# A selective-scan kernel: 64-step blocks for the drive, high channels first, softplus steps spread, delta spread by six reads

## The chip, the cores and the metric

The kernel runs on one core of one Trainium2 chip. The time is device microseconds of one execution. Lower is better.

## The reference

The model has two layers over 8 images of 64 x 64 x 96. The first is a group norm, an input projection to 192 channels and a gate, a 3 x 3 depthwise convolution with SiLU, and a selective scan in four directions (k): along two diagonal orders of the pixels and their reverses. The second is linear attention and a feed-forward layer in quantized arithmetic. The change touches the scan alone:

```python
delta = softplus(dts + dt_projs_bias)            # per k: 192 channels, 4096 steps
def step(hst, inp):                              # hst: 4 x 192 channels x 16 states
    u_t, d_t, B_t, C_t = inp
    hst = hst * exp(d_t[..., None] * A) + (d_t * u_t)[..., None] * B_t[:, :, None, :]
    return (hst, einsum('bkdn,bkn->bkd', hst, C_t))
```

## The kernel before

Each image goes through stages; a barrier of all engines (`rendezvous`) stands between them. The scan stage has four passes, one for each direction, of 8 chunks of T = 512 steps: 256 chunks in all. In a chunk the 192 x 16 states are 3072 rows of 512, cut into 12 *steps* s of 2 x 128 rows. A step takes one group of CW = 32 channels (GROUPS[s], six groups) and half of the 16 states (pr = s // 6; NJ = 4 quadrants of 32 partitions with 2 states, index a, each).

A step s consists of
- `decays` (ScalarE, L650): two exponentials of `delta_rep[:, g, :]`, where delta of the group's 32 channels stands four times, once in each quadrant. It is issued two steps ahead;
- `fill` (TensorE, L856): the drive delta x u x B of the step, by matmuls into two of four PSUM banks. The stationary operand is `du_t` (delta x u, turned so that time lies on partitions), the moving one `b_diag`, in which B stands on a diagonal. It is 32 matmuls, 64 instructions, in tiles of 64 rows by 32 columns. It is issued two steps ahead and waits for the scan of step s - 2, whose banks it writes;
- four `tensor_tensor_scan` (VectorE, L1144), halves of 256 steps for a = 0, 1;
- `save_state` (ScalarE, L632), then the product with C (GpSimdE, L487), which waits for that copy;
- `sum_states` (TensorE, L886), in batches of four steps, into the Y banks 4 and 5. Its place in TensorE's order is SUM_SLOTS.

While chunk ch runs, the next one, nx, is prepared, by calls written by hand into each engine's loop over s: `project` (TensorE, L819, L820: delta before softplus, and B and C), `copy_bc`, `clamp_exp`, `square_log` (ScalarE), `softplus_part` and `times_u` (GpSimdE, L463, L471), `at_least_log` and `make_delta` (VectorE, L1109, L1115), `turn_b`, `turn_du` (TensorE, L829, L838), `save_bt`, `save_du` (ScalarE, L606, L614). Each exists twice, v = 0 for the 64 high channels (DLO:DI) with B and C, v = 1 for the 128 low ones. Each engine works in order, so a call that waits holds up all behind it.

`prepare` is SyncE's list of DMAs for nx, also in order: C to DRAM, B to DRAM by four stores (L368), delta's high rows (L375), the reads of B's first half (L384), C's first half (L391), delta's low rows (L406), then 12 reads of delta (L401, 32 partitions each), B's and C's second halves. In `b_runs` each step's 8 values are 32 bytes of a row of 512 elements, and a shifted window over the rows gives the diagonal. Time is interleaved: block k of a half holds the steps t with t mod 4 = k (`every`).

## Time and profile before

| | us |
|---|---|
| median of 3 runs | 16174.73 (16163.91 to 16176.15) |
| the profiled execution | 16179.37 |
| its span | 16176.9 |

| engine | busy us | share of the span |
|---|---|---|
| TensorE, matmuls | 12939.1 | 80% |
| VectorE | 9552.7 | 59% |
| GpSimdE | 8899.6 | 55% |
| ScalarE | 7503.2 | 46% |

The shares are means over all stages. The scan stage shows in the page's slices as three to four of every five slices, with TensorE at 8, VectorE and GpSimdE at 6 tenths. In the rows below PE is TensorE, PEld its weight loads, DVE VectorE, ACT ScalarE, POOL GpSimdE, SPq the DMA queue of SyncE. L487 is line 487 of the kernel. All on-chip working buffers of the scan are parts of one tensor, `arena`, so rows are told apart by their lines.

### The profile page before, as it was taken

How to read it: one execution, taken by the hardware profiler on the slowest of the kernel's cores; microseconds unless marked ns; L12 is line 12 of the kernel's file. 1: busy time of each engine (PE TensorE's matmuls, PEld its weight loads, DVE VectorE, ACT ScalarE, POOL GpSimd, SP SyncE). 2: the span in 40 equal slices, each digit the busy share in tenths (PEclk: the TensorE clock that was granted, in tenths of full speed). 3: DMA queues.
4: the chain of work that ended last, by engine and by line, in shares of the span. 5: the costliest groups of instructions: out<-in, count | busy, mean ns of one | idle time of the engine just before them, and what ended most of it. 6: DMA issues, size and time to landing. Idle time of an engine off the chain costs nothing.

```text
span 16176.9 us, 551693 instructions
## 1 busy us (share of the span) xinstructions
PE 12939.1 (80%) x223648; PEld 6772.7 (42%) x223648; DVE 9552.7 (59%) x14966; ACT 7503.2 (46%) x14253; POOL 8899.6 (55%) x4341
## 2 busy tenths in 40 slices
PE   7888778887788877888778887788877888778887
PEld 3444434444344443444434444344443444434444
DVE  4666446664466644666446674466744667346673
ACT  4544344443444434445344453444534445344553
POOL 3666336663366633666346672466624667246672
PEclk9999699996899968999699996999969999699996
DMA  3444124441244412444124441344413444134441
GB/s 86 109 109 111 34 71 109 111 108 34 73 107 110 108 35 72 109 111 108 33 76 110 105 110 32 77 108 106 110 33 77 108 105 111 32 78 106 107 110 28
DMA packets 1044001, 1404.93 MB, mean 87 GB/s; under 512 B 461935, under 2 KB 463504, under 8 KB 1041148
## 3 DMA queue, kind: packets, MB, share of 16 engines
q1 hardware_dynamic: 1041660, 1369.95, 33.3%
q8 instruction: 1929, 31.60, 0.9%
q14 instruction: 412, 3.38, 0.1%
HBM read 1235.32 MB, written 134.23 MB: 85 GB/s over the span
## 4 chain that ended last, share of the span: by engine, by line
PE 51%; issue 18%; DVE 16%; ACT 4%; DMA 4%; POOL 4%; DVEq 2%; SPq 1%; POOLq 1%; ACTq 0%
PE ps L856 21%; DVE arena L1144 14%; PE ps L886 7%; PE ps L794 5%; DMA delta_rows<-arena 2%; PE ps L819 2%; PE ps L961 2%; PE ps L960 2%; PE ps L820 2%; POOL arena L463 2%; PE ps L939 2%; ACT arena L650 1%; POOL arena L487 1%; ACT arena L590 1%; DMA arena<-delta_rows 1%
## 5 line engine op out<-in xcount | busy, mean ns | idle before, releaser
L487 POOL TENSOR_TENSOR arena<-arena 128x1024 f32<-128x1024 f32 x3072 | 7282.7, 2383 | 3990.2 <-ACT arena L632 3535.9
L1144 DVE TENSOR_TENSOR_SCAN arena<-arena,ps 128x256 f32<-128x256 f32 x12288 | 7950.2, 720 | 2128.5 <-ACT arena L650 987.6
L856 PE MATMUL ps<-arena 64*32 64x128 f32 x196608 | 6478.8, 407 | 2222.7 <-DVE arena L1144 1614.9
L856 PEld LDWEIGHTS ps<-arena 64*32 64x32 f32 x196608 | 3959.4, 120 | 5099.0 <-issue 4176.2
L650 ACT ACTIVATE arena<-arena,negA 128x512 f32<-128x512 f32 x6144 | 4054.0, 710 | 472.0 <-DMA arena<-delta_rows 298.1
L886 PE MATMUL ps<-arena,gather 128*32 128x512 f32 x12288 | 2092.6, 610 | 28.0 <-POOL arena L487 28.0
L632 ACT ACTIVATE arena<-arena 128x2 f32<-128x2 f32 x2688 | 523.7, 195 | 1723.7 <-DVE arena L1144 1723.6
L463 POOL TENSOR_TENSOR arena<-arena 128x512 f32<-128x512 f32 x512 | 662.8, 1295 | 1070.5 <-ACT arena L589 1070.5
L1109 DVE SCALAR_TENSOR_TENSOR ps<-ps,dtb,arena 128x512 f32<-128x512 f32 x512 | 382.3, 747 | 1456.8 <-ACT arena L590 1456.8
L599 ACT ACTIVATE arena<-ps 32x512 f32<-32x512 f32 x256 | 150.9, 590 | 1684.3 <-PE ps L820 1684.3
L507 POOL TENSOR_TENSOR arena<-arena 128x512 f32<-128x512 f32 (+1 forms) x128 | 159.7, 1268 | 1232.1 <-ACT arena L717 1232.1
L614 ACT ACTIVATE arena<-ps 128x256 f32<-128x256 f32 (+1 forms) x512 | 251.2, 491 | 1223.0 <-PE ps L838 1222.2
L794 PE MATMUL ps<-arena,wconv 96*64 96x512 f32 (+1 forms) x2304 | 777.9, 606 | 47.2 <-POOLq L172 47.2
L886 PEld LDWEIGHTS ps<-arena,gather 128*32 128x32 f32 x12288 | 358.3, 109 | 1035.5 <-issue 868.0
L819 PE MATMUL ps<-u_lo,xw_lo 128*128 (+1 forms) x1024 | 651.6, 722 | 105.8 <-DVEq L172 54.4
L580 ACT ACTIVATE arena<-ps,nb 128x512 f32<-128x512 f32 x512 | 349.2, 682 | 653.6 <-PE ps L820 650.4
L1115 DVE TENSOR_TENSOR arena<-ps,arena 128x512 f32<-128x512 f32 x512 | 350.2, 684 | 446.4 <-POOL arena L463 442.0
L820 PE MATMUL ps<-u_hi,xw_hi 128*128 (+1 forms) x1024 | 559.9, 630 | 0.0
L794 PEld LDWEIGHTS ps<-arena,wconv 96*64 96x64 f32 (+1 forms) x2304 | 303.6, 166 | 515.1 <-issue 515.1
L838 PEld LDWEIGHTS ps<-ident,arena 64*128 64x128 f32 (+1 forms) x2048 | 285.6, 209 | 374.9 <-issue 374.9
L1179 DVE TENSOR_TENSOR arena<-ps,arena 128x384 f32<-128x384 f32 x64 | 35.7, 558 | 663.4 <-PE ps L961 663.4
L838 PE MATMUL ps<-ident,arena 64*128 64x64 f32 (+1 forms) x2048 | 370.7, 303 | 46.2 <-POOL arena L471 46.2
(172 smaller groups left out, 8983.8 us busy)
## 6 DMA issues: line engine op xcount, KB each, us to landing
arena<-b_runs SPq DMA_DIRECT2D x1024, 512.0 KB, 6.3
arena<-delta_rows SPq DMA_DIRECT2D x3072, 128.0 KB, 4.6
arena<-c_rows SPq DMA_DIRECT2D x512, 512.0 KB
delta_rows<-arena SPq DMA_DIRECT2D x256, 256.0 KB, 6.7
delta_rows<-arena SPq DMA_DIRECT2D x256, 128.0 KB, 2.2
arena<-in_x SPq DMA_DIRECT2D x128, 192.0 KB, 3.2
b_runs<-arena SPq DMA_DIRECT2D x1024, 8.0 KB, 1.9
out_tokens<-arena SPq DMA_DIRECT2D x64, 192.0 KB, 2.2
```

Source lines behind the costliest of these rows:

```text
L463: pool.tensor_tensor(t_q, t_e, t_q, ALU.subtract).then_inc(t_done, 1)
L487: pool.tensor_tensor(h, h, c_rep[s // NG], ALU.mult).then_inc(weighted, 1)
L632: act.activation(state[:, 2 * s:2 * s + 2], hst[ch.slot(s)][:, :, col], ACT.Copy).then_inc(state_saved, 1)
L650: act.activation(decay[s % RDA][:, a, :], delta_rep[:, g, :], ACT.Exp, scale=negA[:, ch.k, i:i + 1]).then_inc(decay_ready, 1)
L794: return pe.matmul(to.rearrange("p (r w) -> p r w", w=W), wconv[:, t, channels], xT_img[:, r0:r0 + ROWS, dx:dx + W], start=(t == 0), stop= ...
L819: pe.matmul(bank(HI_BANK + v), xw_lo[:, ch.k, z * P:(z + 1) * P], u_lo[:, ch.dir, cols], start=True, stop=False)
L820: pe.matmul(bank(HI_BANK + v), xw_hi[:, ch.k, z * P:(z + 1) * P], u_hi[:, cols], start=False, stop=True).then_inc(pre_filled, 1)
L838: mm = pe.transpose(bank(HI_BANK + v)[:, k * w:(k + 1) * w], every(du[r, :], k), ident[r, r])
L856: mm = pe.matmul(to, du_t[ch.par][rows, k, g * CW:(g + 1) * CW], runs[rows, j, :, :], start=True, stop=True)
L886: mm = pe.matmul(bank(bk)[row:row + CW, :], gather[:, :], hst[ch.slot(s)][:, a, :], start=(ch.kk == 2 and s < NG and a == 0), stop=(s >= N ...
L1109: dve.scalar_tensor_tensor(to, to, dtb[:, 1 - v, ch.k:ch.k + 1], t_l, ALU.add, ALU.max).then_inc(m_done, 1)
L1144: dve.tensor_tensor_scan(h_out[:, a, cols][:, flip], decay[s % RDA][:, a, cols][:, flip], ps[:, 2 * (s % 2) + half, a * HALF:(a + 1) * HAL ...
```

## The change

- **Blocks.** Block k of a half now holds 64 consecutive steps (`steps` in place of `every`). A fill's matmul writes 64 adjacent PSUM columns for each a, where it wrote every fourth, and reads `b_diag` with a step of 2 elements (order "j t a") where the step was 8. Numbers and sizes of the matmuls of `fill` stay.
- **Turns.** `turn_b` and `turn_du` turn 64 steps at a time with matmuls against the identity in place of transposes: 8 and 2 x 8 of them, for 4 and 2 x 4. B is turned into the free partitions 64 to 127 of bank 5; it was bank 7.
- **B through DRAM.** The stores write the diagonal itself: 8 stores (two halves, four quadrants), each of 64 x 8 pieces of 2 values, where 4 stores wrote 64 x 4 pieces of 8 values. The reads take plain rows; count and size stay.
- **High channels first.** GROUPS becomes 4, 5, 0, 1, 2, 3 in both halves, so the first two steps need only v = 0. The lo half of delta x u is copied in step 0 of the next chunk, and fill 2 waits for it.
- **Softplus.** Its steps move to later and wider places, and the logarithm `t_l` has one buffer for each v.
- **Delta.** One store a part as before, and six reads (one a group) whose source is repeated four times by an outermost dimension of stride 0 and whose target is all 128 partitions.

Left out of the diff: constants, the sizes of a few buffers, the zeroing of the new DRAM tensors, and the index of `t_l`.

```diff
@@ -203,14 +202,15 @@
...
-t_e, t_q, t_l, du, bc_raw = (cv(T) for _ in range(5))
-b_t = cv(NB * NS).rearrange("p (k n) -> p k n", n=NS)
+t_e, t_q, du, bc_raw = (cv(T) for _ in range(4))
+t_l = [cv(T) for _ in range(2)]
+b_t = cv(2 * NB * NS).rearrange("p (h i n) -> p h i n", h=2, n=RUN)
...
-f_dram = [[nc.dram_tensor("b_runs%d%d" % (par, pr), (FLEN,), F32, kind="Internal").ap() for pr in range(NPR)] for par in range(2)]
+f_dram = [nc.dram_tensor("b_runs%d" % par, (2 * FLEN,), F32, kind="Internal").ap() for par in range(2)]
@@ -272,11 +272,12 @@
...
-GROUPS = (0, 1, 2, 3, 4, 5, 2, 3, 0, 1, 4, 5)
-def every(ap, k):
-    return ap.rearrange("p (t k) -> p t k", k=NB)[:, :, k]
+GROUPS = (4, 5, 0, 1, 2, 3) * NPR
+BT_ROWS = slice(DHI, P)
+def steps(h, k):
+    return slice(h * HALF + k * TB, h * HALF + (k + 1) * TB)
@@ -362,26 +363,18 @@
...
-            for pr in range(NPR):
-                for h in range(2):
-                    runs = f_dram[par][pr][h * HALF * PITCH + SKEW:h * HALF * PITCH + SKEW + HALF * PITCH]
-                    sp.dma_start(runs.rearrange("(k t w) -> t k w", t=TB, w=PITCH)[:, :, 0:RUN],
-                                 b_t[h * TB:(h + 1) * TB, :, pr * RUN:(pr + 1) * RUN]).then_inc(b_written, 16)
-            wait_apart(sp, delta_done, ch.n(2, 1))
-            if not ch.early:
-                for g in range(NG // 2):
-                    wait_apart(sp, delta_loaded[g], ch.n(16 * NJ, -16 * NJ))
-            sp.dma_start(delta_dram[par][DLO:DI, :], t_l[ch.r0:ch.r0 + DHI, :]).then_inc(delta_written[0], 16)
+            for h in range(2):
+                for j in range(NJ):
+                    spots = bass.AP(f_dram[par].tensor, f_dram[par].offset + h * FLEN + j * 2 * TB, [[PITCH + 2, TB], [TB * PITCH, NPR * NB], [1, 2]])
+                    sp.dma_start(spots, b_t[BT_ROWS, h, :, 2 * j:2 * j + 2]).then_inc(b_written, 16)
             def load_b(pr):
...
-                wait_apart(sp, b_written, ch.n(16 * 2 * NPR, 16 * 2 * NPR))
+                wait_apart(sp, b_written, ch.n(16 * 2 * NJ, 16 * 2 * NJ))
...
-                    window = f_dram[par][pr][h * HALF * PITCH + SKEW:h * HALF * PITCH + SKEW + TB * (PITCH - RUN)]
-                    window = bass.AP(window.tensor, window.offset, [[PITCH - RUN, TB], [TB * PITCH, NB], [1, PITCH]])
-                    sp.dma_start(b_diag[pr][h * TB:(h + 1) * TB, :, :], window).then_inc(b_loaded[pr], 16)
+                    rows = f_dram[par][h * FLEN + pr * (FLEN // 2):h * FLEN + (pr + 1) * (FLEN // 2)]
+                    sp.dma_start(b_diag[pr][h * TB:(h + 1) * TB, :, :], rows.rearrange("(k t w) -> t k w", t=TB, w=PITCH)).then_inc(b_loaded[pr], 16)
             def load_c(pr):
@@ -390,24 +383,32 @@
...
+            def store_delta(v):
+                wait_apart(sp, delta_done, ch.n(2, v + 1))
+                if not ch.early:
+                    for i in ((0, 1) if v else (2,)):
+                        wait_apart(sp, delta_loaded[i], ch.n(32, -32))
+                if v:
+                    sp.dma_start(delta_dram[par][0:DLO, :], t_l[v]).then_inc(delta_written[v], 16)
+                else:
+                    sp.dma_start(delta_dram[par][DLO:DI, :], t_l[v][ch.r0:ch.r0 + DHI, :]).then_inc(delta_written[v], 16)
             def load_delta(i):
+                v = 0 if i == 2 else 1
...
-                wait_apart(sp, delta_written[0], ch.n(16, 16))
-                if i < 2:
-                    wait_apart(sp, delta_written[1], ch.n(16, 16))
-                rows = delta_dram[par][2 * CW * i:2 * CW * (i + 1), :].rearrange("(g d) t -> d g t", d=CW)
-                for j in range(NJ):
-                    sp.dma_start(delta_rep[j * CW:(j + 1) * CW, 2 * i:2 * i + 2, :], rows).then_inc(delta_loaded[i], 16)
+                wait_apart(sp, delta_written[v], ch.n(16, 16))
+                for g in (2 * i, 2 * i + 1):
+                    sp.dma_start(delta_rep[:, g, :], delta_dram[par][g * CW:(g + 1) * CW, :].unsqueeze(0).to_broadcast([NJ, CW, T])).then_inc(delta_loaded[i], 16)
...
+            store_delta(0)
...
-            wait_apart(sp, delta_done, ch.n(2, 2))
-            sp.dma_start(delta_dram[par][0:DLO, :], t_l).then_inc(delta_written[1], 16)
+            load_delta(2)
+            store_delta(1)
+            load_b(1)
...
-            load_b(1)
-            load_delta(2)
@@ -484,15 +485,15 @@
...
+                if nx and s == 7:
+                    softplus_part(nx, 1)
                 pool.tensor_tensor(h, h, c_rep[s // NG], ALU.mult).then_inc(weighted, 1)
...
-                    if s == 2:
+                    if s == 4:
...
-                    if s == 3:
+                    if s == 6:
...
-                    if s == 5:
-                        softplus_part(nx, 1)
-                    if s == 7:
+                    if s == 8:
@@ -584,10 +585,13 @@
         def square_log(ch, v):
...
-                act.wait_ge(du_done, ch.n(2, v))
-                act.wait_ge(delta_written[1 - v], ch.n(16, 16 * v))
+                act.wait_ge(delta_done, ch.n(2, v))
             act.activation(t_q[:, :], t_e[:, :], ACT.Square, scale=0.5 ** 0.5).then_inc(sq_done, 1)
-            act.activation(t_l[:, :], t_e[:, :], ACT.Ln, bias=one[:, :]).then_inc(ln_done, 1)
+            if not ch.first:
+                act.wait_ge(du_done, ch.n(2, v - 1))
+                for i in ((0, 1) if v else (2,)):
+                    act.wait_ge(delta_loaded[i], ch.n(32, 0))
+            act.activation(t_l[v], t_e[:, :], ACT.Ln, bias=one[:, :]).then_inc(ln_done, 1)
         def copy_bc(ch):
@@ -602,13 +606,13 @@
...
-                act.wait_ge(b_written, ch.n(16 * 2 * NPR, 0))
-            act.activation(b_t, bank(LO_BANK)[:, 0:NB * NS].rearrange("p (k n) -> p k n", n=NS), ACT.Copy).then_inc(bt_saved, 1)
+                act.wait_ge(b_written, ch.n(16 * 2 * NJ, 0))
+            act.activation(b_t[BT_ROWS], bank(Y_BANK + 1)[BT_ROWS, 0:2 * NB * NS].rearrange("p (h i n) -> p h i n", h=2, n=RUN), ACT.Copy).then_inc(bt_saved, 1)
         def save_du(ch, v):
...
-            if not ch.early:
+            if v == 0 and not ch.early:
@@ -659,27 +663,29 @@
...
-                if s == 3 and not ch.first:
-                    kk, c = (ch.kk, ch.c - 1) if kind else (ch.kk - 1, NCH - 1)
-                    save_y(Chunk(ch.b, kk, c))
-                if nx:
-                    if s == 1:
-                        copy_bc(nx)
-                        clamp_exp(nx, 0)
-                    if s == 2:
-                        save_bt(nx)
-                        square_log(nx, 0)
-                    if s == 4:
-                        clamp_exp(nx, 1)
-                    if s == 5:
-                        save_du(nx, 0)
-                        square_log(nx, 1)
-                    if s == 10:
-                        save_du(nx, 1)
+                if nx and s == 10:
+                    save_du(nx, 0)
...
+                if s == 0 and not ch.first:
+                    save_du(ch, 1)
+                if s == 4 and not ch.first:
+                    kk, c = (ch.kk, ch.c - 1) if kind else (ch.kk - 1, NCH - 1)
+                    save_y(Chunk(ch.b, kk, c))
+                if nx:
+                    if s == 2:
+                        copy_bc(nx)
+                        clamp_exp(nx, 0)
+                    if s == 3:
+                        save_bt(nx)
+                    if s == 4:
+                        square_log(nx, 0)
+                    if s == 6:
+                        clamp_exp(nx, 1)
+                    if s == 7:
+                        square_log(nx, 1)
@@ -813,8 +819,6 @@
...
-            if v == 1:
-                pe.wait_ge(bt_saved, ch.n(1, 1))
@@ -823,10 +827,12 @@
...
-                wait_apart(pe, dut_saved, ch.n(2, 0))
+                wait_apart(pe, bt_saved, ch.n(1, 0))
...
-            for k in range(NB):
-                mm = pe.transpose(bank(LO_BANK)[:, k * NS:(k + 1) * NS], every(bc_raw[r, :], k), ident[r, ch.d0:ch.d0 + NS])
+            for h in range(2):
+                for k in range(NB):
+                    to = bank(Y_BANK + 1)[BT_ROWS, h * NB * NS:(h + 1) * NB * NS].rearrange("p (q k n) -> p q k n", k=NB, n=RUN)[:, :, k, :]
+                    mm = pe.matmul(to, bc_raw[r, steps(h, k)], ident[r, ch.d0:ch.d0 + NS].rearrange("p (q n) -> p q n", n=RUN), start=True, stop=True)
...
         def turn_du(ch, v):
@@ -835,25 +841,26 @@
...
-                mm = pe.transpose(bank(HI_BANK + v)[:, k * w:(k + 1) * w], every(du[r, :], k), ident[r, r])
+                for h in range(2):
+                    mm = pe.matmul(bank(HI_BANK + v)[h * TB:(h + 1) * TB, k * w:(k + 1) * w], du[r, steps(h, k)], ident[r, r], start=True, stop=True)
...
         def fill(ch, s):
...
-            if s == 0:
-                wait_apart(pe, dut_saved, ch.n(2, 2))
+            if s in (0, 2):
+                wait_apart(pe, dut_saved, ch.n(2, 1 + s // 2))
...
-                runs = b_diag[pr][:, k, :].rearrange("p (t j a) -> p j a t", j=NJ, a=2)
+                spots = b_diag[pr][:, k, :].rearrange("p (j t a) -> p j a t", j=NJ, a=2)
...
-                        to = ps[j * CW:(j + 1) * CW, 2 * (s % 2) + h, :].rearrange("p (a t k) -> p a t k", a=2, k=NB)[:, :, :, k]
-                        mm = pe.matmul(to, du_t[ch.par][rows, k, g * CW:(g + 1) * CW], runs[rows, j, :, :], start=True, stop=True)
+                        to = ps[j * CW:(j + 1) * CW, 2 * (s % 2) + h, :].rearrange("p (a k t) -> p a k t", a=2, k=NB)[:, :, k, :]
+                        mm = pe.matmul(to, du_t[ch.par][rows, k, g * CW:(g + 1) * CW], spots[rows, j, :, :], start=True, stop=True)
...
         def pre(ch):
@@ -905,13 +912,13 @@
...
-                    if s == 1:
+                    if s == 2:
...
-                    if s == 4:
+                    if s == 8:
...
-                    if s == 9:
+                    if s == 10:
@@ -1145,10 +1152,13 @@
...
-                    if s in (2, 6):
-                        at_least_log(nx, s // 6)
-                    if s in (3, 7):
-                        make_delta(nx, s // 7)
+                    if s == 5:
+                        at_least_log(nx, 0)
+                    if s == 6:
+                        make_delta(nx, 0)
+                    if s == 8:
+                        at_least_log(nx, 1)
+                        make_delta(nx, 1)
```

## Rows read from the trace of the kernel before

**Rows 1.** Page, DMA issues: target<-source, times, KB each, us from issue to landing
```profile
delta_rows<-arena SPq DMA_DIRECT2D x256, 128.0 KB, 2.2
...
b_runs<-arena SPq DMA_DIRECT2D x1024, 8.0 KB, 1.9
```

**Rows 2.** Stretch, us; busy PE PEld DVE ACT POOL (x), PE clock, DMA share, GB/s
```profile
4500.00:5000.00 500.00, 419.14 (x8665) 209.81 (x8648) 346.00 (x536) 248.75 (x497) 344.70 (x166) 0.98 0.43 110
```

**Rows 3.** Groups by line and form, 4500 to 5000: busy us, mean ns | idle before
```profile
L1144 DVE TENSOR_TENSOR_SCAN arena<-arena,ps 128x256 f32<-128x256 f32 x494 | 320.2, 722 | 82.2 <-ACT arena L650 46.0 <-PE ps L856 19.8 <-PE ps L886 12.5
...
L487 POOL TENSOR_TENSOR arena<-arena 128x1024 f32<-128x1024 f32 x124 | 294.1, 2384 | 151.9 <-ACT arena L632 137.9 <-DVE arena L1144 13.4
...
L856 PE MATMUL ps<-arena 64*32 64x128 f32 x7921 | 261.4, 407 | 77.2 <-DVE arena L1144 61.3 <-issue 15.9
...
L650 ACT ACTIVATE arena<-arena,negA 128x512 f32<-128x512 f32 x250 | 164.8, 710 | 11.2 <-DVE arena L1144 6.1 <-DMA arena<-delta_rows 5.1
...
L463 POOL TENSOR_TENSOR arena<-arena 128x512 f32<-128x512 f32 x21 | 27.2, 1297 | 4.0 <-ACT arena L589 4.0
...
L1109 DVE SCALAR_TENSOR_TENSOR ps<-ps,dtb,arena 128x512 f32<-128x512 f32 x21 | 15.7, 746 | 57.6 <-ACT arena L590 57.6
...
L614 ACT ACTIVATE arena<-ps 128x512 f32<-128x512 f32 x10 | 6.0, 597 | 38.4 <-PE ps L838 38.4
...
L606 ACT ACTIVATE arena<-ps 128x64 f32<-128x64 f32 x10 | 2.2, 224 | 10.3 <-PE ps L829 10.3
```

**Rows 4.** Timeline, two chunks: start us, us, engine, line, what, instructions merged
```profile
4273.90 2.07 PE L856 MATMUL ps<-arena 64*32 64x128 f32 x64 [1.33 <-DVE arena L1144]
...
4275.90 1.12 PE L819 MATMUL ps<-u_lo,xw_lo 128*128 x2
...
4277.81 2.08 PE L856 MATMUL ps<-arena 64*32 64x128 f32 x64
...
4601.62 1.06 PE L886 MATMUL ps<-arena,gather 128*32 128x512 f32 x8
...
4602.61 2.07 PE L856 MATMUL ps<-arena 64*32 64x128 f32 x64
...
4603.02 10.32 DVE L1144 TENSOR_TENSOR_SCAN arena<-arena,ps 128x256 f32<-128x256 f32 x16 [0.89 <-ACT arena L650]
...
4611.38 0.75 PE L838 MATMUL ps<-ident,arena 128*128 128x128 f32 x4
```

**Rows 5.** Inside one fill: L856 by source, the next batch of sums, a 0.24 us window
```profile
L856 PE MATMUL ps<-arena x64: 392/409/413, 4602.6 to 4604.3; 64*32 64x128 f32 x64
...
4602.07 0.61 PE L886 MATMUL ps<-arena,gather 128*32 128x512 f32 x4
...
4606.02:4606.26 0.24, 0.24 (x16) 0.18 (x8) 1.00 0.52 179
```

**Rows 6.** Timeline of SyncE's DMA issues, one chunk (duration is that of the issue)
```profile
4630.87 2.60 SPq L368 DMA_DIRECT2D b_runs<-arena  x4
...
4638.88 1.25 SPq L384 DMA_DIRECT2D arena<-b_runs  x2
...
4648.66 0.55 SPq L391 DMA_DIRECT2D arena<-c_rows  x1
...
4650.56 0.35 SPq L406 DMA_DIRECT2D delta_rows<-arena  x1
...
4657.87 4.21 SPq L401 DMA_DIRECT2D arena<-delta_rows  x8
```

**Rows 7.** Stretches, columns as in rows 2: B's reads, C's read, after idleness of TensorE
```profile
4639.00:4645.00 6.00, 4.96 (x75) 2.38 (x74) 6.00 (x10) 4.61 (x9) 3.81 (x3) 1.00 0.85 199
...
4652.00:4656.00 4.00, 3.06 (x104) 1.73 (x88) 4.00 (x7) 1.43 (x3) 4.00 (x4) 1.00 0.31 107
...
4622.00:4624.00 2.00, 2.00 (x59) 1.54 (x42) 0.18 (x1) 0.00 (x0) 0.17 (x1) 0.50 0.28 104
```

**Rows 8.** Timeline at the start of a loop iteration
```profile
4476.89 1.14 PE L856 MATMUL ps<-arena 64*32 64x128 f32 x26 [7.12 <-issue]
```

More of the change, by code:

```diff
@@ L39 @@
 PITCH = TB * RUN
-SKEW = (TB - 1) * RUN
-FLEN = T * PITCH + 2 * PITCH
+FLEN = T * PITCH
 NSCAN = 4 * NSTEP
@@ L339, in _ @@
             for par in range(2):
-                for pr in range(NPR):
-                    sp.dma_start(f_dram[par][pr].rearrange("(p f) -> p f", p=P), zeros).then_inc(zeroed, 16)
-            sp.wait_ge(zeroed, 16 * 2 * NPR)
+                for h in range(2):
+                    sp.dma_start(f_dram[par][h * FLEN:(h + 1) * FLEN].rearrange("(p f) -> p f", p=P), zeros).then_inc(zeroed, 16)
+            sp.wait_ge(zeroed, 16 * 2 * 2)
             sp.drain().then_inc(phase_done, 1)
@@ L364, in prepare @@
                     wait_apart(sp, bt_saved, ch.n(1, 1))
-                    for pr in range(NPR):
-                        for h in range(2):
-                            runs = f_dram[par][pr][h * HALF * PITCH + SKEW:h * HALF * PITCH + SKEW + HALF * PITCH]
-                            sp.dma_start(runs.rearrange("(k t w) -> t k w", t=TB, w=PITCH)[:, :, 0:RUN],
-                                         b_t[h * TB:(h + 1) * TB, :, pr * RUN:(pr + 1) * RUN]).then_inc(b_written, 16)
-                    wait_apart(sp, delta_done, ch.n(2, 1))
-                    if not ch.early:
-                        for g in range(NG // 2):
-                            wait_apart(sp, delta_loaded[g], ch.n(16 * NJ, -16 * NJ))
-                    sp.dma_start(delta_dram[par][DLO:DI, :], t_l[ch.r0:ch.r0 + DHI, :]).then_inc(delta_written[0], 16)
+                    for h in range(2):
+                        for j in range(NJ):
+                            spots = bass.AP(f_dram[par].tensor, f_dram[par].offset + h * FLEN + j * 2 * TB, [[PITCH + 2, TB], [TB * PITCH, NPR * NB], [1, 2]])
+                            sp.dma_start(spots, b_t[BT_ROWS, h, :, 2 * j:2 * j + 2]).then_inc(b_written, 16)
                     def load_b(pr):
@@ L470, in times_u @@
                     cols = bass.ds(ch.t0, T)
-                    pool.tensor_tensor(du, t_l, u_lo[:, ch.dir, cols] if v else u_hi[:, cols], ALU.mult).then_inc(du_done, 1)
+                    pool.tensor_tensor(du, t_l[v], u_lo[:, ch.dir, cols] if v else u_hi[:, cols], ALU.mult).then_inc(du_done, 1)
                 def pre(ch):
@@ L646, in decays @@
                     if pr == 0:
-                        act.wait_ge(delta_loaded[g // 2], ch.n(16 * NJ, 16 * NJ))
+                        act.wait_ge(delta_loaded[g // 2], ch.n(32, 32))
                     for a in range(2):
@@ L837, in turn_du @@
                     for k in range(NB):
-                        mm = pe.transpose(bank(HI_BANK + v)[:, k * w:(k + 1) * w], every(du[r, :], k), ident[r, r])
+                        for h in range(2):
+                            mm = pe.matmul(bank(HI_BANK + v)[h * TB:(h + 1) * TB, k * w:(k + 1) * w], du[r, steps(h, k)], ident[r, r], start=True, stop=True)
                     mm.then_inc(du_turned, 1)
@@ L1108, in at_least_log @@
                     to = bank(HI_BANK + v)
-                    dve.scalar_tensor_tensor(to, to, dtb[:, 1 - v, ch.k:ch.k + 1], t_l, ALU.add, ALU.max).then_inc(m_done, 1)
+                    dve.scalar_tensor_tensor(to, to, dtb[:, 1 - v, ch.k:ch.k + 1], t_l[v], ALU.add, ALU.max).then_inc(m_done, 1)
                 def make_delta(ch, v):
@@ L1114, in make_delta @@
                     dve.wait_ge(t_done, ch.n(2, v + 1))
-                    dve.tensor_tensor(t_l, bank(HI_BANK + v), t_q, ALU.max).then_inc(delta_done, 1)
+                    dve.tensor_tensor(t_l[v], bank(HI_BANK + v), t_q, ALU.max).then_inc(delta_done, 1)
                 def pre(ch):
```

## The prediction

> **What bounds the kernel now.** I read the by-form groups of one scan stretch first. [rows 2, 3] come from 500 us of it: TensorE is busy 419 us, the scans of VectorE 320, GpSimdE's weighting 294, the exponentials of ScalarE 165. 494 scans at 48 a chunk make 10.3 chunks, so a chunk takes 48.6 us. The reader is to see there that a fill of the drive (L856, 64 instructions a step) takes 261 of the 419 us of TensorE. Next, the timeline for slots [rows 4]: a fill holds TensorE 2.00 us (4273.90 to 4275.90), a batch of sums 0.99 (4601.62 to 4602.61), a projection 1.91 (4275.90 to 4277.81), a pair-of-four turn 0.75; VectorE runs four steps of scans in 10.32 us, 2.58 a step. TensorE then has, a chunk, 12 x 2.00 + 6 x 0.99 + 2 x 1.91 + turns about 2 + carry about 2 = 38 us, VectorE 12 x 2.58 + 2 x 1.45 = 33.9, GpSimdE 12 x 2.38 + 4 x 1.3 = 33.8 [rows 3]. TensorE is the fullest and sits behind a double buffer: a fill of step s+2 starts only when scan s is done. At the start of a loop iteration it also stands 7.12 us with nothing to run [rows 8]; that is two chunks in eight. No engine is saturated, so the other half of the reading is the DMA queue [rows 6, 7].
>
> **The fill.** Its 64 matmuls start in rounds of eight, one round each 0.24 us: first and last start are 1.7 us apart over eight rounds, and in a window of 0.24 us sixteen are in flight [rows 5]. That is 1.9 ns a column for 128 columns. The sums, 512 columns each into contiguous columns, start four (4601.62 [rows 4]) and then four more 0.45 us later (4602.07 [rows 5]), 0.9 ns a column, and last 0.61 us where a fill's last 409 ns [rows 5]. So a fill runs at half the rate of a sum. The old fill writes every fourth PSUM column and reads SBUF with a step of 8 elements; the new one writes 64 adjacent columns and reads with a step of 2. I take the sum's rate for it: 128 x 0.9 = 0.115 us, 0.13 with the seam between rounds, 8 x 0.13 + 0.08 = 1.15 us. Bounds: 0.95 (no seam) and 2.00 (nothing gained). I take 1.15, because a sum's 610 ns less its stream of 450 plus 115 is 275, and a fill's matmul lasts 409: it is slow in its stream, not in its start. TensorE loses 12 x 0.85 = 10.2 us a chunk. The Trainium skill, SBUF — State Buffer, "Door 1" (its note on cachelines), says that SBUF lines are 16 bytes and PSUM lines 8, and that non-contiguous PSUM patterns slow matmuls significantly; the trace's factor of two agrees.
>
> **The turns.** Transposes (one instruction) become two-instruction matmuls into half the columns. B: 8 for 4; delta-u: 16 for 8. Now 0.75 us each at most [rows 4]; the new ones lie between 0.75 and 1.5, taken 1.1: +1 us a chunk, inside the 10 freed. B's turn also leaves bank 7, so the second projection no longer waits for its copy: nothing, since two steps lie between them.
>
> **Softplus steps.** The same operations one to three steps later: no work is added; VectorE does 0.75 + 0.7 us in one piece after step 8 [rows 3]. The logarithm gets two buffers, which removes the wait for the store. What counts is that delta is finished later in the chunk (hi after step 6, lo after step 8, before 3 and 7).
>
> **DMAs.** B's diagonals take 8 stores in place of 4. Four now cost SP 2.60 us to issue [rows 6], 0.65 each, and land in 1.9 [rows 1]. Eight at 0.65 are 5.2; each has 512 pieces of 8 bytes for 256 of 32, so the bound above is 1.3 each. 12 delta reads become 6; they save SP about 3 us. What matters is where they run. The read of C is shaped the same way (outermost dimension 4 in DRAM, 128 partitions in SBUF). It keeps 0.31 of the engines busy at 107 GB/s over four windows, with some foreign traffic in them [rows 7], that is four engines of sixteen, for 5.0 us (512 KB). The lo store issued just behind it at 4650.56 lets the reads go only at 4657.87, 7.3 us [rows 6], against 2.2 for the hi store [rows 1]. I price the six reads like C: 256 KB on four engines, 2.5 us by the row, 2.6 with seams, 15.6 us a chunk on the same four as C's 10.4. The bounds for a pair are 5.2 and 2.6 (199 GB/s, as B's reads do on all engines [rows 7]). The Trainium skill, DMA: Bandwidth & Descriptors, "Rules for kernel authors", says that a leading broadcast of c copies confines a DMA to c engines. By that rule the trace agrees for C, and this is the rule that speaks against the change.
>
> **The chain of a new chunk.** Zero is the start of its scan 2. TensorE: projection, partly at the low clock, 2.3; fill 1.15, sums 1.0, fill 1.15, sums 1.0, turn 0.7; copy of B's turn 0.22 [rows 3] and semaphores, 0.35: 7.65. Eight stores 5.2 and 1.5 more to land: 14.3. Reads of B's first half, 1 MB at 199 GB/s: issued by 14.8, done 20.1. On the four engines then the hi store 0.3, C's first half 5.2: 25.6. Delta's hi pair was issued at 22, done 30.8, known 31.8. Two exponentials (0.71 each [rows 3]): the next chunk's scan 0 starts at 33.2. VectorE alone would be there at 10 x 2.58 + 2.9 = 28.7, so it stands 4.5. ScalarE stands in its own queue for that read; behind it stand the state copies, for which GpSimdE waits. Then on the four engines: lo store 0.3, B's second half 2.6, delta groups 0 and 1, 5.2: 38.9, known 40.1. Exponentials 1.4, then in ScalarE's order the copy of delta-u's lo half 0.6 [rows 3], for which fill 2 now waits, then the fill. After 5 us of idleness it runs at the low clock: between 4622 and 4624, after such a gap, the clock was 0.50 [rows 7]. So the fill is 2.0; with semaphores 0.4 scan 2 starts at 44.5. The reads for groups 2 and 3 end at 45.3, in time for scan 4 near 49. The four engines carry 10.4 + 15.6 + 7.8 for B + 3 for stores = 37 us, so they are not the bound by volume; the chain is.
> The iteration-start gap of 7.12 falls where TensorE now idles 5 us anyway; what is left, 3 us on 2 of 8 chunks, adds 0.75. Mean 45.25 against 48.6, 3.35 x 256 chunks = 858 us saved. Before each image's first scan 2, where nothing hides them, two pairs of reads are 2 x 2.6 = 5 us slower, 40 in eight images. The profiled execution took 16179.4 us, 5 above the median 16174.7. 16179 - 858 + 40 - 5 = 15356, about **15360**.
>
> **Rivals.**
> (B) The delta reads use all sixteen engines, or more than the price above says. Speaks for it: the reads cover 128 partitions and B's, into 64, reach 199 GB/s on all [rows 7]. Against: C's shape. A pair takes 2.6, the hi pair is in time, lo known at 33.3, exponentials, copy, fill: 36.5; the iteration gap is no longer hidden, +2: 38.5. 10.1 x 256 = 2586 saved: 13600. The Trainium skill, SBUF — State Buffer, "Door 1", has 32 partitions reach half the ports that 128 reach, by which wider reads would gain as here; no run here shows ports.
> (C) The fill doesn't get faster: 30 ns from start to start (0.24 us over 8) would be the pace of issue. For: no stretch of this trace issues faster for long. Against: the eight of a round start together, then nothing starts [rows 5]. The chain grows by 0.85 x 2 to 46.2, the gap isn't hidden (+2), and TensorE's own 39.5 us fill the rest: 48.2 to 49.5, so 16100 to 16450, 16250 in the middle. TensorE: Matmul & The Clock Gate, "Back-to-back issue gap" and Part 1, in the Trainium skill, gives a floor of about 25 ns from start to start; 64 x 25 would be 1.6 us a fill, between this and the forecast.
> (D) The other side: the stores of B. They sit on SP in front of everything. Each us that they take longer is a us of the chain. From 1.05 us each (3.2 us over the eight) the gain is gone; at 1.3, twice today's for twice the pieces, the chunk takes 45.25 + 5.2 = 50.45, and 1.85 x 256 + 40 more than now is 16690. For: twice the pieces, each a quarter as long. Against: C's read with half as many pieces as B's costs SP 0.56 against 0.63 [rows 6], so pieces hardly count.
> (E) The reorder doesn't reach the path at all (a stall that I can't see in old rows stays): 16175.
>
> **How the numbers follow.** The chain 50%, its own range 14700 to 16150; B 15%; C 15%; D 15%; E and others 5%. Likeliest 15360. From 13800 to 16900 leaves out most of B and the far end of D, some 18%. What this kernel's measurement can tell from no change is about 0.2%. Faster: 45 from the chain and all of B, 0.60. Within 0.2%: 0.08, from the chain's end, C and E. Slower: 0.32, from C, D and the rest.
>
> **What would show it.** Right: a fill's matmuls near 290 ns and its slot near 1.15; a DMA share of 0.25 to 0.3 in stretches of 5 us behind C's read; ScalarE's exponentials waiting for delta reads about 5 us twice a chunk; TensorE idle most before fill 2, with a low clock after. Wrong: fill matmuls still 409 ns (C), a share near 1 during delta reads (B), SP busy over 8 us with B's stores (D). The sum fails most easily at the four-engine price, which enters three times, and at the low clock: were it low for the whole chunk, TensorE's 28 us would come near 56.

## The result, and the profile after

The changed kernel takes 17004.3 us (median of 4 runs, 16995.7 to 17038.7) against 16175.4 us beside it: ratio 1.0517, interval 1.0498 to 1.0535. It is slower by 829 us where 15360 was forecast, and lies beyond the range, which ended at 16900. The profiled execution took 16995.7 us. Ratios and medians are of executions in the faster of two states; one execution of run 9 below (18009.4 us, granted clock 0.575) was in the slower.

| | before | after |
|---|---|---|
| span, us | 16176.9 | 16993.9 |
| TensorE, busy us | 12939.1 | 11368.4 |
| VectorE | 9552.7 | 9590.2 |
| GpSimdE | 8899.6 | 8837.7 |
| ScalarE | 7503.2 | 7510.5 |
| TensorE clock, mean | 0.897 | 0.757 |

TensorE lost 1571 us of work, the others kept theirs, and the span grew. So the time is in waits. Lines of the page after: the slices of the clock, the chain that ended last, two groups (busy, mean ns | idle before), four DMA rows (KB, us to landing).

```profile
PEclk8877677776777767777677776777767777677876
...
DMA 43%; PE 30%; SPq 13%; issue 5%; ACT 4%; POOL 2%; DVE 1%; POOLq 1%; ACTq 0%; DVEq 0%
DMA delta_rows<-arena 26%; DMA arena<-delta_rows 13%; SPq L369 8%; PE ps L863 6%; PE ps L800 5%; DMA b_runs<-arena 4%; PE ps L893 3%; PE ps L823 3%; SPq L377 2%; SPq L402 2%; PE ps L968 2%; PE ps L967 2%; PE ps L824 2%; PE ps L835 2%; PE ps L946 1%
...
L863 PE MATMUL ps<-arena 64*32 64x128 f32 x196608 | 4259.1, 311 | 4654.2 <-ACT arena L618 3387.4
L654 ACT ACTIVATE arena<-arena,negA 128x512 f32<-128x512 f32 x6144 | 4065.7, 710 | 5085.5 <-DMA arena<-delta_rows 4574.6
...
arena<-b_runs SPq DMA_DIRECT2D x1024, 512.0 KB, 9.0
...
delta_rows<-arena SPq DMA_DIRECT2D x256, 256.0 KB, 12.4
b_runs<-arena SPq DMA_DIRECT2D x2048, 4.0 KB
delta_rows<-arena SPq DMA_DIRECT2D x256, 128.0 KB, 5.4
```

The chain is now 43% transfers and 13% SyncE's issuing. The *hi* and *lo store* are SyncE's stores of delta's high (128 KB) and low (256 KB) channels to DRAM. The hi store lands after 5.4 us for 2.2 in [rows 1]. The lo store takes 12.4; on the page before it took 6.7:

```profile
delta_rows<-arena SPq DMA_DIRECT2D x256, 256.0 KB, 6.7
```

The stretch that answers to [rows 2], and its longest waits (us in total, times, longest):

```profile
4500.00:5000.00 500.00, 332.46 (x8456) 183.81 (x8456) 322.26 (x497) 237.46 (x477) 316.92 (x154) 0.79 0.40 100
```
```profile
ACT arena L654 <- DMA arena<-delta_rows: 170.7, 22, 11.7
PE ps L863 <- ACT arena L618: 138.2, 10, 16.3
...
DVE arena L1151 <- PE ps L863: 97.9, 20, 8.8
...
DVE arena L1151 <- ACT arena L654: 63.4, 12, 7.4
```

ScalarE's exponentials wait 170.7 us of 500 for delta's reads where L650 in [rows 3] waited 5.1. TensorE waits 138.2 us, once a chunk, up to 16.3, for the copy of delta-u's lo half that stands behind those exponentials in ScalarE's order.

One chunk on SyncE's queue, answering to [rows 6]. Its scan 2 starts at 4665.71, that of the next chunk at 4718.59.

```profile
4670.82 0.33 SPq L364 DMA_DIRECT2D c_rows<-arena  x1
4675.27 6.50 SPq L369 DMA_DIRECT2D b_runs<-arena  x8
4683.51 2.35 SPq L377 DMA_DIRECT2D arena<-b_runs  x2
4686.18 0.49 SPq L394 DMA_DIRECT2D delta_rows<-arena  x1
4686.93 0.54 SPq L384 DMA_DIRECT2D arena<-c_rows  x1
4691.25 1.10 SPq L402 DMA_DIRECT2D arena<-delta_rows  x2
4692.69 0.33 SPq L392 DMA_DIRECT2D delta_rows<-arena  x1
4696.19 1.27 SPq L377 DMA_DIRECT2D arena<-b_runs  x2
4705.29 2.63 SPq L402 DMA_DIRECT2D arena<-delta_rows  x4
4710.85 0.51 SPq L384 DMA_DIRECT2D arena<-c_rows  x1
4723.09 0.34 SPq L364 DMA_DIRECT2D c_rows<-arena  x1
```

From C's store to the next is 52.3 us here, 51.9 on the mean of the six that start with it; 3.3 more than the 48.6 of before, times 256 chunks, is 845, about the whole loss of 829. The whole traces say the same: within an image the mean is 51.7 for 48.3. The first step of each image stands out, 47.6 to 50.9 us for 32.2 to 32.8, some 130 us in eight images. The gap at the start of a loop iteration [rows 8] no longer adds, since every chunk now stands longer than that. What ended last, and what it released (chain of waits, then the timelines of ScalarE, TensorE and VectorE):

```profile
4679.44 1.66 SPq L369
4681.14 2.29 DMA b_runs<-arena
...
4686.18 4.97 DMA delta_rows<-arena
...
4692.69 12.51 DMA delta_rows<-arena
...
4705.89 8.28 DMA arena<-delta_rows
```
```profile
4704.55 1.33 ACT L654 ACTIVATE arena<-arena,negA 128x512 f32<-128x512 f32 x2 [10.14 <-DMA arena<-delta_rows]
...
4714.20 1.33 ACT L654 ACTIVATE arena<-arena,negA 128x512 f32<-128x512 f32 x2 [6.90 <-DMA arena<-delta_rows]
```
```profile
4716.45 1.96 PE L863 MATMUL ps<-arena 64*32 64x128 f32 x64 [14.67 <-ACT arena L618]
```
```profile
4718.59 2.67 DVE L1151 TENSOR_TENSOR_SCAN arena<-arena,ps 128x256 f32<-128x256 f32 x4 [8.08 <-PE ps L863]
```

And the DMA engines meanwhile, columns as in [rows 2]:

```profile
4687.00:4691.00 4.00, 1.95 (x105) 1.70 (x98) 3.71 (x6) 2.00 (x5) 4.00 (x4) 0.90 0.88 196
4693.00:4697.00 4.00, 3.00 (x72) 1.74 (x72) 4.00 (x8) 0.52 (x2) 4.00 (x3) 0.50 0.41 157
4699.00:4703.00 4.00, 2.78 (x88) 1.77 (x80) 0.00 (x0) 0.00 (x0) 0.00 (x0) 1.00 1.05 194
4706.00:4713.00 7.00, 0.00 (x0) 0.00 (x0) 4.51 (x8) 1.29 (x3) 4.64 (x2) 0.50 0.27 91
4714.00:4716.00 2.00, 0.00 (x0) 0.00 (x0) 0.00 (x0) 1.80 (x4) 0.00 (x0) 0.50 0.26 102
```

Nearly all DMA engines work while B's halves are read (0.88 and 1.05); in the two stretches between 4706 and 4716 only a share of 0.26 to 0.27 works, and nothing computes on TensorE. In the Trainium skill, DMA: Bandwidth & Descriptors, "Rules for kernel authors", a leading broadcast of c copies keeps a DMA to at most c engines; the share agrees for c = 4 of 16.

### The profile page after: what moved, and what is told of

Read it like the earlier page. It is cut to its first block, busy times and chain, and to the rows that moved or that the text cites. A ratio compares the mean times of both kernels' runs of the same rounds, so it can differ in the third digit from the quotient of the medians.

```text
span 16993.9 us, 569259 instructions
## 1 busy us (share of the span) xinstructions
PE 11368.4 (67%) x232864; PEld 6446.3 (38%) x232864; DVE 9590.2 (56%) x14966; ACT 7510.5 (44%) x14253; POOL 8837.7 (52%) x4341
## 4 chain that ended last, share of the span: by engine, by line
DMA 43%; PE 30%; SPq 13%; issue 5%; ACT 4%; POOL 2%; DVE 1%; POOLq 1%; ACTq 0%; DVEq 0%
DMA delta_rows<-arena 26%; DMA arena<-delta_rows 13%; SPq L369 8%; PE ps L863 6%; PE ps L800 5%; DMA b_runs<-arena 4%; PE ps L893 3%; PE ps L823 3%; SPq L377 2%; SPq L402 2%; PE ps L968 2%; PE ps L967 2%; PE ps L824 2%; PE ps L835 2%; PE ps L946 1%
## 5 line engine op out<-in xcount | busy, mean ns | idle before, releaser
L863 PE MATMUL ps<-arena 64*32 64x128 f32 x196608 | 4259.1, 311 | 4654.2 <-ACT arena L618 3387.4
L863 PEld LDWEIGHTS ps<-arena 64*32 64x32 f32 x196608 | 3304.8, 117 | 6553.2 <-issue 6545.6
L893 PE MATMUL ps<-arena,gather 128*32 128x512 f32 x12288 | 2288.0, 679 | 22.7 <-POOL arena L490 22.7
L823 PE MATMUL ps<-u_lo,xw_lo 128*128 (+1 forms) x1024 | 820.3, 895 | 54.4 <-DVEq L171 54.4
L824 PE MATMUL ps<-u_hi,xw_hi 128*128 (+1 forms) x1024 | 640.3, 712 | 0.0
L845 PE MATMUL ps<-ident,arena 64*64 64x64 f32 (+1 forms) x8192 | 486.5, 264 | 43.6 <-POOL arena L472 43.6
L845 PEld LDWEIGHTS ps<-ident,arena 64*64 64x64 f32 (+1 forms) x8192 | 385.8, 146 | 327.6 <-issue 327.6
L824 PEld LDWEIGHTS ps<-u_hi,xw_hi 128*128 128x128 f32 x1024 | 263.5, 257 | 386.0 <-issue 386.0
L583 ACT ACTIVATE arena<-arena,c 128x512 f32<-128x512 f32 x512 | 370.1, 723 | 16.7
## 6 DMA issues: line engine op xcount, KB each, us to landing
delta_rows<-arena SPq DMA_DIRECT2D x256, 256.0 KB, 12.4
```

The costliest lines, as they stand in the source:

```text
L823: pe.matmul(bank(HI_BANK + v), xw_lo[:, ch.k, z * P:(z + 1) * P], u_lo[:, ch.dir, cols], start=True, stop=False)
L824: pe.matmul(bank(HI_BANK + v), xw_hi[:, ch.k, z * P:(z + 1) * P], u_hi[:, cols], start=False, stop=True).then_inc(pre_filled, 1)
L845: mm = pe.matmul(bank(HI_BANK + v)[h * TB:(h + 1) * TB, k * w:(k + 1) * w], du[r, steps(h, k)], ident[r, r], start=True, stop=True)
L863: mm = pe.matmul(to, du_t[ch.par][rows, k, g * CW:(g + 1) * CW], spots[rows, j, :, :], start=True, stop=True)
L893: mm = pe.matmul(bank(bk)[row:row + CW, :], gather[:, :], hst[ch.slot(s)][:, a, :], start=(ch.kk == 2 and s < NG and a == 0), stop=(s >= N ...
```

## The experiments

Three theories. **T1**: the chunk is as long as the chain of transfers on SyncE's queue, and the four-engine reads stretch it. **T2**: the softplus steps stand too late. **T3**: B's eight stores on SyncE cost the time (the prediction's D). Of twelve runs, 1 to 6 and 9 to 12 are medians of three to four executions, 7 and 8 single ones. The diffs leave out the semaphore counts and increments that go with an edit. A quotient of times is against the kernel before on the same chip. One us of chunk is 256 us of time.

**1. Twelve delta reads in the changed kernel.**
```diff
-for g in (2 * i, 2 * i + 1):
-    sp.dma_start(delta_rep[:, g, :], delta_dram[par][g * CW:(g + 1) * CW, :].unsqueeze(0).to_broadcast([NJ, CW, T]))
+rows = delta_dram[par][2 * CW * i:2 * CW * (i + 1), :].rearrange("(g d) t -> d g t", d=CW)
+for j in range(NJ):
+    sp.dma_start(delta_rep[j * CW:(j + 1) * CW, 2 * i:2 * i + 2, :], rows)
```


> The changed kernel with the delta reads of before (12 reads of 32 partitions in place of six of 128), all else as changed. Theory 1 (the period of a chunk is the chain of DMAs, and the six reads are long because each runs on four of sixteen engines): the two pairs in the chain take 2.6 us in place of 5.2 to 8, the low clock before fill 2 goes, a chunk falls from 51.9 to 41 to 44 us, and the kernel to 14200 to 15000 us. Theory 2 (delta comes late because its softplus steps were moved): nothing in the reads matters, 16800 or more. Theory 3 (the eight stores of B and what they put on SyncE): at most 1 us a chunk, 16700 or more.

Measured 15395.8 us, 0.9525 (0.9509 to 0.9541): 1608 us less than the changed kernel, from this edit alone. T1 has the sign and most of the size, though it had asked for still more (15000 at most): C's read stays on four engines, and the lo store still landed only after 7.7 us.

**2. The kernel before with the six reads**, the same edit backwards.

> The kernel before with the six reads of the changed kernel alone: old blocks, old stores of B, old places of the softplus steps. Theory 1: ScalarE waits for delta some 2 to 6 us longer in each chunk, 16700 to 17700 us. Theories 2 and 3: within 50 us of before, about 16175.

Measured 17024.8 us, 1.053 (1.0512 to 1.0547): 850 us lost with neither late softplus steps nor eight stores. T2 and T3 aren't needed for a loss. Here the lo store lands no later than in the kernel before (6.5 us for 6.7), and the loss is in the reads themselves. Page, then one read of a low group in the chain that ended last:

```profile
delta_rows<-arena SPq DMA_DIRECT2D x256, 256.0 KB, 6.5
...
4697.60 8.57 DMA arena<-delta_rows
```

Runs 1 and 2 part the change: without the six reads, the rest of it gains 779 us on the kernel before; the six reads cost 850 there and 1608 in the changed kernel. Which part of the rest brings the 779 us, no run tells.

**3. C read in four pieces of 32 partitions**, in the changed kernel.
```diff
-sp.dma_start(c_rep[pr], rows.rearrange("(j a) t -> j (a t)", a=2).unsqueeze(1).to_broadcast([NJ, CW, 2 * T]))
+for j in range(NJ):
+    sp.dma_start(c_rep[pr][j * CW:(j + 1) * CW, :], rows[2 * j:2 * j + 2, :].rearrange("a t -> (a t)").unsqueeze(0).to_broadcast([CW, 2 * T]))
```


> The changed kernel with each read of C cut into four reads of 32 partitions, whose outermost dimension is 32; delta reads as changed. Theory 1: C leaves the four engines, of which it takes 10.4 us a chunk; its first half stands ahead of delta's high pair in the chain, so a chunk gets 2 to 4 us shorter, 16000 to 16500 us. Theories 2 and 3: no change, about 17000; if SyncE's issue time were what binds, the six issues more make it slower.

Measured 16716.1 us, 1.0336 (1.0319 to 1.0354), 1.1 us a chunk; less than T1 asked. Its chain says why. The lo store landed 4.1 us sooner, and the read behind it, now close behind B's second half, took 10.72 us for 8.28 (chain of run 3):

```profile
4668.32 8.44 DMA delta_rows<-arena
...
4677.45 10.72 DMA arena<-delta_rows
```

**4. Edits 1 and 3 together.**

> Both: delta and C read in pieces of 32 partitions. Theory 1: a chunk near 38 to 40 us, close to the 34 us of VectorE and GpSimdE alone, 13600 to 14200 us, faster than both kernels. Theories 2 and 3: no better than 16800.

Measured 15170.9 us, 0.938 (0.9364 to 0.9396). The lo store now lands after 2.5 us (page):

```profile
delta_rows<-arena SPq DMA_DIRECT2D x256, 256.0 KB, 2.5
```

It is faster than both kernels, and above the expectation. ScalarE still waited 93.0 us of 500 for delta: B's second half, delta's lo groups and C, 2.5 MB, were issued within 9 us and shared all sixteen engines just as they were needed.

**5. and 6. B's second half after delta's lo groups**, in the changed kernel and in kernel 4.
```diff
 store_delta(1)
-load_b(1)
 load_delta(0)
 load_delta(1)
+load_b(1)
```


> The changed kernel with one thing moved: SyncE issues the B runs' second half (1 MB) after the four delta reads of the low channels, not ahead of them. T1 (the chunk is as long as the chain of transfers: B stores, B half 1, C's first half, delta's three parts): the 1 MB leaves the window between the C read and the low store's landing, so the low store (which lands 12.5 us after issue in the changed kernel, with B half 2 beside it) lands 2 to 4 us sooner and the chunk shortens by 2 to 5 us of 52: 15500 to 16500 us. T2 (the softplus steps lie too late in the chunk): nothing changes, 16950 to 17050. T3 (the eight B stores on SyncE cost the time): nothing changes either. A way to be wrong for T1: B half 2 then becomes the late one for step 4's fill (PE waits for b_loaded), and the time stays near 17000 or rises.

Run 5 measured 16550.2 us, 1.0241 (1.0224 to 1.0259), 1.8 us a chunk, 50 us above T1's range. The lo store landed after 9.5 us, still behind the reads of C and of delta's hi groups.

> The kernel with twelve delta reads and C read in four pieces a half (15171 us, a chunk of 44 us), and the B runs' second half issued after the eight delta reads of the low channels. In the run before this, VectorE's late step waited for delta(0), which landed 6.6 to 7 us after issue while B half 2 (1 MB), delta (1 MB) and C (0.5 MB) went through all sixteen engines at 220 to 240 GB/s. T1: delta(0) lands 2.5 to 4 us sooner, the chunk shortens by 2 to 4 us, 14000 to 14700 us. T2 (softplus steps late) and T3 (B stores on SyncE): no gain, 15100 to 15250; under T2 the delta store itself would be what the reads wait for.

Run 6 measured 14495.8 us, 0.8965 (0.8951 to 0.898), within T1's range. The same move is worth 2.6 us a chunk once the four-engine reads are gone. The chain that ended last is no longer one of transfers:

```profile
PE 58%; issue 15%; DVE 9%; DMA 5%; ACT 4%; SPq 4%; POOL 3%; DVEq 1%; POOLq 1%; ACTq 0%
```

The lo store on the pages of runs 5, 3 and 1, where 12.4 stood for the changed kernel:

```profile
delta_rows<-arena SPq DMA_DIRECT2D x256, 256.0 KB, 9.5
...
delta_rows<-arena SPq DMA_DIRECT2D x256, 256.0 KB, 8.5
...
delta_rows<-arena SPq DMA_DIRECT2D x256, 256.0 KB, 7.7
```

**7. and 8. Which of the fill's two strides counts.** Run 7 writes PSUM as before (step 4), run 8 reads the B runs as before (step 8); each changes which numbers the drive gets, not how many.
```diff
 # run 7
-to = ps[...].rearrange("p (a k t) -> p a k t", a=2, k=NB)[:, :, k, :]
+to = ps[...].rearrange("p (a t k) -> p a t k", a=2, k=NB)[:, :, :, k]
 # run 8
-spots = b_diag[pr][:, k, :].rearrange("p (j t a) -> p j a t", j=NJ, a=2)
+spots = b_diag[pr][:, k, :].rearrange("p (t j a) -> p j a t", j=NJ, a=2)
```


> The changed kernel with the drive's matmuls writing PSUM with a step of 4 elements as the kernel before did (so the drive has its time steps permuted, and the output is not the reference's); the moving operand is read as in the changed kernel (adjacent pairs, 8 bytes apart). It tells which of the two strides made a matmul of the fill 270 ns instead of 409. If it is the PSUM step: mean of one matmul back at 390 to 410 ns, slot near 2.0 us. If it is the moving operand's step: it stays at 265 to 280 ns and 1.1 us. The total may rise by a few per cent in the first case (T1: the fills are not on the chain but for one, so by under 1.5%), and not at all in the second.

> The changed kernel with the drive's matmuls reading the B runs with a step of 8 elements as the kernel before did (so they take other numbers than they should, and the output is not the reference's), and writing adjacent PSUM elements as in the changed kernel. If the moving operand's step set the rate: mean of one matmul back at 390 to 410 ns. If the PSUM step did: it stays at 265 to 280 ns.

The fill's group over 500 us, run 7, then run 8 with its stretch, its chain that ended last and its lo store (page):

```profile
L863 PE MATMUL ps<-arena 64*32 64x128 f32 x7464 | 159.2, 308 | 167.2 <-ACT arena L618 130.8 <-DVE arena L1151 36.4
```
```profile
L863 PE MATMUL ps<-arena 64*32 64x128 f32 x7488 | 244.0, 407 | 94.3 <-ACT arena L618 71.3 <-DVE arena L1151 23.1
```
```profile
4500.00:5000.00 500.00, 400.82 (x8556) 207.97 (x8548) 335.32 (x512) 235.45 (x473) 326.55 (x157) 0.94 0.40 104
...
PE 49%; DMA 29%; issue 7%; DVE 4%; SPq 4%; ACT 4%; POOL 2%; POOLq 1%; DVEq 0%; ACTq 0%
...
delta_rows<-arena SPq DMA_DIRECT2D x256, 256.0 KB, 7.6
```

Only the step of the moving operand in SBUF counts: 407 ns with it, 308 without (309 in the changed kernel over the same 500 us; the means mix fills at both clock levels). And run 8, with the slow fill, took 16970 us for run 7's 17001, in single runs: in the changed kernel the fast fill is worth nothing that shows. TensorE is busy 401 us for 332, and its clock was 0.94 for 0.79. Its chain is another one, though: it runs over TensorE first, then from `make_delta` of the low channels to the lo store, which goes out later and lands after 7.6 us. So with the slow fill another chain, of about the same length, ends last, and the store's landing time is not by itself what the chunk pays.

**9. The start of the chain one step earlier**: ScalarE's copy and first exponential, TensorE's turn of b and ScalarE's copy of it.
```diff
-if s == 2:          # ScalarE: copy_bc, clamp_exp; TensorE: turn_b
+if s == 1:
...
-if s == 3:          # ScalarE: save_bt
+if s == 2:
```


> The changed kernel with the start of the chain one step earlier: ScalarE's copy of the projection and its exponential, PE's turning of b and ScalarE's copy of the turned b stand at steps 1, 1 and 2, not 2, 2 and 3 (the other softplus steps stay). T1 (the chunk is the chain from the projection through B's stores and all reads to delta(0), every piece queued behind the one before it on SyncE): the whole chain starts one step, some 3 us, sooner and the chunk shortens by 2 to 3 us of 52: 16200 to 16500 us. T2 (the softplus steps set the time): the stores of delta don't move, so no change, 16900 to 17050. T3 (only the eight stores' issue time matters): their number is the same, but the rest moves with them, so T3 alone gives what T1 gives.

Ratio 1.0306 (1.0265 to 1.0347), about 16660 us, 1.3 us a chunk, half of what was expected and 160 us above T1's range. B's stores start 7.06 us after scan 2 (4661.17 to 4668.23) for 9.56, so the start did move by 2.5. Part was given back at once: from the first store's issue to the next read's it took 9.2 us for 8.2, and the hi store then landed after 6.5 us (median) for 5.4. T2 alone would have had no change.

**10. Half of B's stores from ScalarE's queue**, in the changed kernel.
```diff
-for h in range(2):
+for h in range(1):      # SyncE; the other four behind ScalarE's save_bt
...
+    act.dma_start(spots, b_t[BT_ROWS, 1, :, 2 * j:2 * j + 2])
```


> The changed kernel with four of the eight B stores issued from ScalarE's queue right behind its copy of the turned b, the other four from SyncE. T1 and T3: SyncE's issue of B's stores takes 3.3 us instead of 6.5 (0.62 to 0.64 us each), the last store lands up to 2.5 us sooner, the chunk shortens by 1.5 to 2.6 us less what ScalarE's 2.6 us of issuing delays: 16300 to 16700 us. If the stores were not on the chain (or ScalarE's issue costs more there than it saves): 17000 or above.

Measured 16711.1 us, 1.0341 (1.0323 to 1.0358), 1.1 us a chunk, 11 us above the range: the stores are on the chain. T1 and T3 expected the same here, so this run doesn't part them; that is done by run 2.

**11. Edits 1, 3, 5, 9 and 10 together; 12. the same without 10.**

> All five edits: twelve delta reads, C read in pieces, B half 2 last, half of B's stores from ScalarE, the start of the chain one step earlier. From 14496 us (the first three; a chunk of 39.3 us, in which SyncE waits for ScalarE's copies and VectorE is busy 79%) the last two can take off 0 to 2.5 us a chunk if SyncE's chain is still what ends last, and nothing if ScalarE's order does. T1: 13850 to 14450 us. If ScalarE's issue of four stores (2.6 us) falls on what is now the tightest engine order: 14500 to 14900.

> The kernel with twelve delta reads, C in pieces and B half 2 last (14496 us), with the start of the chain one step earlier and all B stores still on SyncE. With half of B's stores on ScalarE as well the time was 15018 us, and ScalarE stood 4.03 us at its four stores, with VectorE's scans behind it. If ScalarE's issuing was what cost the 520 us: this kernel is at 14350 to 14600. If the earlier copy is what costs (ScalarE stands at step 1 until the projection's matmul is done, 6.6 us there, with the exponentials of step 3 behind it): 14800 to 15050.

(The chunk of kernel 6, given there as 39.3 us, is 51.9 - 9.8 = 42.1; VectorE's softplus instructions had been counted among the scans.)

Run 11: 15018.2 us, 0.929 (0.9268 to 0.9312), slower than kernel 6 and above both of its ranges. Run 12: 14234.2 us, 0.8796 (0.8781 to 0.8811), the fastest. So ScalarE's four stores cost 784 us here, 3.1 us a chunk, where they had gained 293 in run 10. ScalarE's timeline in run 11:

```profile
4660.35 0.27 ACT L612 ACTIVATE arena<-ps 64x128 f32<-64x128 f32 x1 [0.37 <-PE ps L844]
4660.73 4.03 ACTq L619 DMA_DIRECT2D b_runs<-arena  x4
4664.86 0.21 ACT L645 ACTIVATE arena<-arena 128x2 f32<-128x2 f32 x1 [4.24 <-DVE arena L1160]
```

Its exponentials stand 4.03 us behind its own issuing. In run 10 this issuing took 2.65 to 2.96 us, and ScalarE waited 136.6 us of 500 for delta anyway; in run 11 it takes 3.65 to 4.23 where transfers no longer bound the chunk. The earlier start (run 12 against 6) gains 262 us, more than expected (14350 at best). Stretch of run 12, columns as in [rows 2]:

```profile
4500.00:5000.00 500.00, 388.52 (x10439) 217.70 (x10423) 403.51 (x624) 294.77 (x583) 391.91 (x191) 0.89 0.54 127
```

VectorE is busy 404 of 500 us, GpSimdE 392.

## Why the prediction was wrong

The mechanism was the forecast one: the chunk is as long as SyncE's chain of transfers, with the delta reads on four engines. The sizes were not. With scan 2 as zero (forecast as in the prediction's chain, measured in the chunk shown):

| | forecast | measured |
|---|---|---|
| B's first store issued | 7.65 | 9.56 |
| stores landed | 14.3 | 17.7 |
| hi store landed | 22 | 25.4 |
| delta hi known | 31.8 | 38.8 |
| delta(0) known | 40.1 | 48.5 |
| next scan 2 | 44.5 | 52.9 |

- **The fill: right** in rate, wrong in reason and worth. A slot at the full clock is 1.12 us for 1.15 (8 x 0.13 + 0.08 is in fact 1.12), its matmuls 270 to 302 ns for 275 forecast. "The trace's factor of two agrees" was said of the note in the Trainium skill, SBUF — State Buffer, "Door 1", on non-contiguous PSUM patterns as well as on SBUF lines; run 7 shows that a PSUM step of 4 costs nothing here, against that note, and run 8 that the SBUF step is all of it. The 10.2 us a chunk that TensorE lost were expected partly on the chain; run 8 shows that they bring nothing that a single run can tell. Rival C falls.
- **Start of the chain: 1.9 us too short.** The projection was taken as 2.3, "partly at the low clock"; in the chunk shown both pairs ran there (0.50 from 4665.5 to 4669.2), 2.00 and 1.71 us, after the wait ahead of fill 2. The fill behind them took 1.38 for 1.15. The turn took 1.04 for 0.7, though the section on the turns had taken 1.1.
- **B's stores: 1.5 too short.** Issue took 6.50 us for 5.2 (mostly 0.62 to 0.64 each, the seventh 1.66), and the last landed 1.66 after the end of issue for 1.5 (the chain's 2.29 holds its own issue). At 0.81 us each they stay under the 1.05 from which rival D was to decide. The result is on D's side, not by D's mechanism; runs 9 and 10 show that the stores are on the chain.
- **The failed step: the transfers behind one another.** The four-engine price itself was right: a share of 0.26 to 0.27 and 91 to 102 GB/s where such reads ran alone. Rival B falls; what it drew from "Door 1" of the Trainium skill, SBUF — State Buffer, that wider reads would gain, run 1 shows the other way round for this shape. But I priced the transfers by their own volume, one after another. Delta hi was known 13.4 us after its store landed, for 9.8: B's second half came in on all sixteen engines while it was read. That half was also taken too cheap, 2.6 us where the first, of the same 1 MB, has 5.3; at the 194 GB/s of the stretch above it is some 5.4, an estimate. And I gave the lo store 0.3 us on the four engines; it lay in the queue behind C's and delta's reads and landed after 12.51 us, with SyncE waiting for it and all low reads behind SyncE. It measured 12.4 us in the changed kernel, and less with each neighbour gone: 9.5 without B's half close behind it (run 5), 8.5 without C's four-engine read (run 3), 7.7 without delta's (run 1), 2.5 without either (run 4). That [rows 6] had shown 7.3 us for this store behind one such read, and that I quoted it, was the warning: with three four-engine reads in the queue I should have let it grow, not shrink. What the chunk pays is when the low reads can go, 39.6 us after scan 2 where the forecast had 33.7 (38.9 less a pair's 5.2).
- **The last piece: right**, 4.4 us, the low clock included (a fill of 1.96 after 14.67 us of waiting; the row it was taken from had 2.91 ahead of it, not 5).
- **Softplus steps (T2): no cost in the changed kernel that a run shows.** The lo delta was done at 4691.3 and its store issued at 4692.69, behind SyncE's issue of the hi reads. With the slow fill of run 8 the store waits for that step (done at 4624.87, store issued at 4625.11), so there is little to spare. No run moved delta's steps alone.
- **The iteration gap** is hidden, more fully than forecast (0.75 a chunk was put down for it, none is seen). Image starts lost some 130 us, not 40; no run tells how much of it is the two pairs of reads.
- **The range.** All misses have one sign, 1.9 + 1.5 + 3.6 + 1.4 = 8.4 us in the chunk shown; 5.0 of them lie in delta's store and reads, each priced by its own bytes. The bounds for a pair of reads were 2.6 and 5.2, with the price taken as the end above; a chain of queued pieces has no such end. The chance for "slower" came from C, D and the rest, and none from the forecast's own mechanism, whose range ended at 16150: 3.4 us more on the chain were enough.

What is open: how much of the 13.4 us is B's half and how much C's rest, since runs 3 and 5 move other pieces too; and why of run 3's 3.9 us at the lo store only 1.1 a chunk is left. In its trace the read behind the store shares the engines from 4682.81 on with C's second half, now on all sixteen (share 0.59 and 0.54, 0.26 just before); no run parts them.

## What to carry to other kernels

Where one queue issues stores and the reads that wait for them, price a chain by what is ahead in the queue and close behind, not by volumes: a narrow read ahead of a small store costs the store's landing. Fewer, wider DMAs are no gain when their leading dimension is a broadcast of four; here twelve reads of 32 partitions beat six of 128 by 1608 us. And work saved on the fullest engine is worth what the chain lets through: see first what the chunk waits for.
